# Late key products of a recurrence from turned keys, with their sums made by TensorE

## The reference, cut to what matters

```python
def ff_step(W, inp):                       # z of every row, known before the recurrence
    qt, kt, vt, bt = inp
    v_old = einsum('bhij,bhj->bhi', W, kt)
    W = W + (bt * (vt - v_old))[..., :, None] * kt[..., None, :]
    return (W, einsum('bhij,bhj->bhi', W, qt))

def rec_step(carry, inp):
    R, h = carry
    zt, kt, vt, bt = inp
    q_rec = softmax(h)                     # over the 32 of each head
    v_old = einsum('bhij,bhj->bhi', R, kt)
    R = R + (bt * (vt - v_old))[..., :, None] * kt[..., None, :]
    h = zt + einsum('bhij,bhj->bhi', R, q_rec)
    return ((R, h), h)
```

## Time and profile before

| | |
|---|---|
| time, median of 3 runs | 637.33 us (637.17 to 638.97) |
| time of the profiled execution | 636.17 us |
| its span | 634.3 us |
| TensorE busy | 565.3 us (89%) |
| VectorE busy | 428.2 us (68%) |
| ScalarE busy | 352.2 us (56%) |
| GpSimd busy | 349.7 us (55%) |
| recurrence, copy of state 0 to copy of state 15 | 262.54 to 439.13 us |

### The profile page before, as it was taken

One profiled execution on the slowest core, in us unless ns is written; L12 is line 12 of the kernel. 1 busy time (PEld: TensorE's weight loads), 2 busy tenths in 40 slices (PEclk: granted clock), 3 DMA queues, 4 the chain that ended last, 5 costly groups with the idle time before them and its releaser, 6 DMA issues.

```text
span 634.3 us, 12534 instructions
## 1 busy us (share of the span) xinstructions
PE 565.3 (89%) x4562; PEld 429.6 (68%) x4562; DVE 428.2 (68%) x1092; ACT 352.2 (56%) x915; POOL 349.7 (55%) x469
## 2 busy tenths in 40 slices
PE   7987999999999786679788878999999999999996
PEld 3556777778435675458777768787567778786686
DVE  4942663423877787799899878998414987766534
ACT  1272444444687674226688867770565577757530
POOL 2597563311450776788999899984366430001435
PEclk9998999999999998898999989999899999999998
DMA  8000000000000434200000000000000000000000
GB/s 281 7 1 1 2 0 1 1 1 1 1 1 2 71 81 67 78 0 2 2 1 1 1 2 1 2 1 0 2 1 1 3 2 2 1 2 2 9 9 17
DMA packets 10860, 10.43 MB, mean 16 GB/s; under 512 B 6000, under 2 KB 9840, under 8 KB 10544
## 3 DMA queue, kind: packets, MB, share of 16 engines
q1 hardware_dynamic: 8080, 7.54, 4.4%
q0 software_dynamic: 2144, 1.75, 1.7%
q10 hardware_dynamic: 576, 0.35, 0.3%
HBM read 5.77 MB, written 0.52 MB: 10 GB/s over the span
## 4 chain that ended last, share of the span: by engine, by line
PE 58%; DVE 17%; POOL 9%; ACT 7%; issue 4%; DMA 4%; SPq 1%; DVEq 0%; POOLq 0%; ACTq 0%
PE bank L1267 8%; PE bank L1347 8%; PE bank L1255 6%; PE bank L1612 5%; PE bank L1571 5%; DVE bank L2061 3%; DVE features L2055 2%; PE bank L1519 2%; PE bank L1658 2%; PE bank L1338 2%; PE bank L1307 2%; DMA coefs<-features 2%; POOL rstd L383 2%; PE bank L1317 2%; DVE features L2031 1%
## 5 line engine op out<-in xcount | busy, mean ns | idle before, releaser
L1347 PE MATMUL bank<-ident,features 128*128 128x128 f32 x604 | 80.7, 284 | 11.8 <-DVE features L2031 6.5
L1347 PEld LDWEIGHTS bank<-ident,features 128*128 128x128 f32 x604 | 71.1, 148 | 19.2 <-DVE features L2031 12.1
L855 ACT ACTIVATE G<-bank,cols 128x512 f32<-128x512 f32 x64 | 43.9, 686 | 54.3 <-PE bank L1255 54.3
L590 POOL TENSOR_TENSOR features<-UV,coefs 128x1024 f32<-128x1024 f32 (+3 forms) x36 | 59.6, 1672 | 2.7 <-DVE UV L2018 2.7
L1267 PE MATMUL bank<-weights,G 128*128 128x128 f32 x512 | 60.9, 278 | 0.0
L1267 PEld LDWEIGHTS bank<-weights,G 128*128 128x128 f32 x512 | 59.6, 195 | 0.0
L1255 PE MATMUL bank<-xs,weights 128*128 128x512 f32 x128 | 57.8, 594 | 0.9 <-ACT xs L846 0.9
L2031 DVE TENSOR_TENSOR features<-UV,bank 128x1024 f32<-128x1024 f32 (+3 forms) x68 | 55.6, 861 | 1.3 <-PE bank L1347 0.6
L390 POOL TENSOR_SCALAR rstd<-mv 128x4 f32<-128x4 f32 x8 | 1.5, 193 | 91.4 <-DVE mv L402 91.4
L940 ACT ACTIVATE xs<-UV,coefs 128x32 f32<-128x32 f32 x232 | 50.3, 308 | 0.0
L940 ACT ACTIVATE sx<-UV,coefs 128x32 f32<-128x32 f32 x200 | 43.4, 309 | 0.0
(11 more groups left out here) (356 smaller groups left out, 1397.2 us busy)
## 6 DMA issues: line engine op xcount, KB each, us to landing
weights<-in_w SPq DMA_DIRECT2D x2, 1024.0 KB, 9.4
features<-in_tok SPq DMA_DIRECT2D x1, 768.0 KB, 5.9
weights<-in_ew SPq DMA_DIRECT2D x4, 128.0 KB, 3.2
weights<-in_ew SPq DMA_DIRECT2D x2, 256.0 KB, 3.0
coefs<-G POOLq DMA_DIRECT2D x16, 25.5 KB, 5.0
rows<-in_rows SPq DMA_DIRECT2D x1, 384.0 KB, 6.3
out_h<-H SPq DMA_DIRECT2D x3, 128.0 KB, 2.0
coefs<-G SPq DMA_DIRECT2D x14, 25.5 KB, 5.0
```

The lines of the kernel that those rows point to most:

```text
L590: pool.tensor_tensor(out, u, co, ALU.mult).then_inc(s["held_p"], 1)
L855: act.activation(G[:, 4 * (w % 2) + f, :], up_bank(f)[:], ACT.Gelu, bias=col("b1", 4 * i + f)).then_inc(s["tok_gelu"], 1)
L1347: last = mm(out[:, P * k:P * k + P], x[:, P * k:P * k + P], ident[:], is_transpose=True, start=first and k == 0, stop=last_ and k == n - 1 ...
```

## The change

The eight late products are made from turned data. TensorE turns keys 4 to 11, one in each of steps 1 to 8 (`turn_keys_late`, two transposes into bank 0), and ScalarE copies each into SBUF (`turned_out`). In steps 10 to 15 the exponential is turned and copied in the same way. GpSimd multiplies the turned keys by the turned exponential; the 32 columns of a head are now 32 partitions. TensorE adds them with `key_sums`: for each product eight multiplications in which the product is the stationary operand and `heads4`, a block of ones for each head, 4 columns wide, is the moving one. VectorE no longer sums these products. It multiplies the sums by the reciprocal straight out of PSUM, in pieces (`shares`), and reads the late pieces last but one. `FIRST` becomes 4 instead of 2 in steps 11 to 14, and `SUMS_WARM` is smaller in steps 10, 12 to 15.

```diff
-FIRST = [min(t + 1, CH if t < 10 else 2) for t in range(T)]
+FIRST = [min(t + 1, 2 if t in (10, 15) else CH) for t in range(T)]
...
-SUMS_WARM = [0, 0, 3, 3] + [6] * 7 + [0] + [6] * 3 + [13]
+SUMS_WARM = [0, 0, 3, 3] + [6] * 6 + [3, 0, 3, 3, 0, 8]
+KEY_TURNS = 8
...
+def turns_until(t):
+    return 2 * NC + (t if t <= KEY_TURNS else KEY_TURNS + max(0, t - KEYS + 1))
...
 # GpSimd, key_products(t)
-                    pool.wait_ge(s["h_exp"], exps_of(t + 1))
+                    pool.wait_ge(s["rk_turned"], turns_until(t))
-                    pool.tensor_tensor(PD[:, j, :].rearrange("p (r x) -> p r x", r=CH), RK[:, CH * j:CH * j + CH, :],
-                                       expS[:].unsqueeze(1).broadcast_to([P, CH, HB]), ALU.mult)
+                    pool.tensor_tensor(PD[:, j, :].rearrange("p (r x) -> p r x", r=CH), keysT[j - 1],
+                                       expT.unsqueeze(1).broadcast_to([P, CH, HB]), ALU.mult)
...
 # ScalarE
+            def turned_out(t, out):
+                act.wait_ge(s["rk_T"], turns_until(t))
+                act.activation(out, bankKT, ACT.Copy).then_inc(s["rk_turned"], 1)
...
                 if t + 1 < T:
                     query_row(t + 1)
+                if 1 <= t <= KEY_TURNS:
+                    turned_out(t, keysT[(t - 1) // CH][:, (t - 1) % CH, :])
+                elif t >= KEYS:
+                    turned_out(t, expT)
+                if t + 1 < T:
                     half = {9: 2, 10: 2, 11: 3}.get(t, OWN[t + 1] // 2)
                     own_rows(t + 1, 0, half)
...
 # TensorE
+            def turn_keys_late(t):
+                x = RK[:, CH + t - 1, :] if t <= KEY_TURNS else expS
+                pe.wait_ge(s["e_sub"], t)
+                if t >= KEYS:
+                    pe.wait_ge(s["h_exp"], exps_of(t + 1))
+                for n in range(2):
+                    last = nc.tensor.transpose(bankKT[:, P * n:P * n + P], x[:, P * n:P * n + P], ident[:])
+                last.then_inc(s["rk_T"], 1)
+
+            def key_sums(t, j):
+                n = key_pieces(t).index(j)
+                pe.wait_ge(s["o_add"], t)
+                pe.wait_ge(s["key_p"], keys_until(t) + n + 1)
+                for r in range(CH):
+                    for k in range(2):
+                        x = HB * r + P * k
+                        last = mm(bankKS[j - 1][:, NH * r + 4 * k:NH * r + 4 * k + 4], PD[:, j, x:x + P], heads4,
+                                  start=True, stop=True)
+                last.then_inc(s["gram_mm"], 1)
...
                 own_reads(t)
+                if 1 <= t <= KEY_TURNS or t >= KEYS:
+                    turn_keys_late(t)
                 queries(t)
...
                 other_reads(t)
+                if t == 12:
+                    pe.wait_ge(s["o_add"], t)
+                    warm(SUMS_WARM[t])
                 if t + 1 < T:
                     held(t + 1)            # key_sums(t, 1) inside it, ahead of the third piece, for t = 11, 12
                     turn_held(t + 1)
-                if SUMS_WARM[t]:
+                if SUMS_WARM[t] and t != 12:
                     pe.wait_ge(s["o_add"], t)
                     warm(SUMS_WARM[t])
+                if t not in (11, 12):
+                    for j in key_pieces(t):
+                        key_sums(t, j)
                 read_out("rec", t, reads_of("rec", t))
...
 # VectorE, read_coefficients(t): shares(lo, hi, sums) multiplies by the reciprocal
-                for n, j in enumerate(key_pieces(t)):
-                    dve.wait_ge(s["key_p"], keys_until(t) + n + 1)
-                    summed(j)
-                ch.settle()
-                cr = bankCR[:, 0:t + 1, :]
-                ch(dve.tensor_tensor(cr, cr, smallv[:, 5, 0:NH].unsqueeze(1).broadcast_to([P, t + 1, NH]), ALU.mult))
+                k1 = CH * (len(key_pieces(t)) + 1)
+                for lo, hi in ((0, CH), (k1, t + 1)) if k1 > CH else ((0, t + 1),):
+                    shares(lo, hi, bankCR[:, lo:hi, :])
...
 # VectorE, step(t)
-                products("rec", t, reads_of("rec", t))
+                part = reads_of("rec", t)
+                late = len(key_pieces(t))
+                products("rec", t, part[:len(part) - late - 1])
+                for n, j in enumerate(key_pieces(t)):
+                    dve.wait_ge(s["gram_mm"], NH * NG + keys_until(t) + n + 1)
+                    shares(CH * j, CH * j + CH, bankKS[j - 1].rearrange("p (r h) -> p r h", r=CH))
+                ch.settle()
+                products("rec", t, part[len(part) - late - 1:])
...
+            ch(dve.tensor_reduce(heads4, ident[:].rearrange("p (h k) -> p h k", h=4), AX_X, ALU.add))
```

More of the change, by code:

```diff
@@ L71, in pieces @@
     return [(r, min(r + step, n)) for r in range(0, n, step)]
-FIRST = [min(t + 1, CH if t < 10 else 2) for t in range(T)]
+FIRST = [min(t + 1, 2 if t in (10, 15) else CH) for t in range(T)]
 def last_row_alone(n):
-    return pieces(n - 1) + [(n - 1, n)] if n > 1 else [(0, 1)]
+    if n <= KEYS:
+        return pieces(n - 1) + [(n - 1, n)] if n > 1 else [(0, 1)]
+    cuts = pieces(n - 1)
+    late = [(CH * j, CH * j + CH) for j in key_pieces(n - 1)]
+    return [c for c in cuts if c not in late] + late + [(n - 1, n)]
 def read_pieces():
@@ L88, in read_pieces, with key_pieces @@
     return out
+KEYS = 10
+KEYS2 = 14
+def key_pieces(t):
+    return [j for j, lo in ((1, KEYS), (2, KEYS2)) if t >= lo]
 READS = read_pieces()
@@ L110, in helds_of @@
     return [(i, r0, r1) for i, (x, r0, r1) in enumerate(HELDS) if x == t]
-SUMS_WARM = [0, 0, 3, 3] + [6] * 7 + [0] + [6] * 3 + [13]
-KEYS = 10
-KEYS2 = 14
+SUMS_WARM = [0, 0, 3, 3] + [6] * 6 + [3, 0, 3, 3, 0, 8]
+KEY_TURNS = 8
 def keys_until(t):
     return max(0, t - KEYS) + max(0, t - KEYS2)
-def key_pieces(t):
-    return [j for j, lo in ((1, KEYS), (2, KEYS2)) if t >= lo]
+def turns_until(t):
+    return 2 * NC + (t if t <= KEY_TURNS else KEY_TURNS + max(0, t - KEYS + 1))
 def exps_of(t):
@@ L239, in build @@
         bankER = bank[3][:, 0:HB]
+        bankKT = bank[0][:, HB:2 * HB]
+        bankKS = [bank[1][:, 128:160], bank[5][:, HB:HB + 32]]
+        keysT = [b.rearrange("p (r x) -> p r x", r=CH) for b in (w1f[:, 1024:2048], SX[:, 2320:3344])]
+        expT = FT[:, 12288:12544]
+        heads4 = smallv[:, 6, 8:12]
         tok = KKf[:, 0:N].bitcast(I32)
@@ L607, in key_products @@
                 if t >= KEYS:
-                    pool.wait_ge(s["h_exp"], exps_of(t + 1))
+                    pool.wait_ge(s["rk_turned"], turns_until(t))
                 for j in key_pieces(t):
-                    pool.tensor_tensor(PD[:, j, :].rearrange("p (r x) -> p r x", r=CH), RK[:, CH * j:CH * j + CH, :],
-                                       expS[:].unsqueeze(1).broadcast_to([P, CH, HB]), ALU.mult).then_inc(s["key_p"], 1)
+                    pool.tensor_tensor(PD[:, j, :].rearrange("p (r x) -> p r x", r=CH), keysT[j - 1],
+                                       expT.unsqueeze(1).broadcast_to([P, CH, HB]), ALU.mult).then_inc(s["key_p"], 1)
             def expert_bias(k):
@@ L1353, in held @@
                 for i, r0, r1_ in helds_of(t):
+                    if t in (12, 13) and r0 == 2 * CH:
+                        key_sums(t - 1, 1)
                     pe.wait_ge(s["held_p"], i + 1)
@@ L1379, in read_out @@
                     last.then_inc(s["read_mm"], 1)
+            def turn_keys_late(t):
[16 more added lines that the diff above has]
+                last.then_inc(s["gram_mm"], 1)
             def turn_state(t):
                 pe.wait_ge(s["hs_saved"], t + 1)
+                if t:
+                    pe.wait_ge(s["rk_turned"], turns_until(t))
                 if t:
@@ L2075, in read_coefficients, with shares @@
                         ch(dve.reciprocal(smallv[:, 5, 0:NH], smallv[:, 4, 0:NH]))
-                for n, j in enumerate(key_pieces(t)):
-                    dve.wait_ge(s["key_p"], keys_until(t) + n + 1)
-                    summed(j)
                 ch.settle()
-                cr = bankCR[:, 0:t + 1, :]
-                ch(dve.tensor_tensor(cr, cr, smallv[:, 5, 0:NH].unsqueeze(1).broadcast_to([P, t + 1, NH]), ALU.mult))
+                k1 = CH * (len(key_pieces(t)) + 1)
+                for lo, hi in ((0, CH), (k1, t + 1)) if k1 > CH else ((0, t + 1),):
+                    shares(lo, hi, bankCR[:, lo:hi, :])
                 ch.settle()
+            def shares(lo, hi, sums):
+                ch(dve.tensor_tensor(bankCR[:, lo:hi, :], sums,
+                                     smallv[:, 5, 0:NH].unsqueeze(1).broadcast_to([P, hi - lo, NH]), ALU.mult))
             def row_stats(t):
```

## The result

The changed kernel takes 652.28 us (median of 4 runs, 648.92 to 655.47), the one before 637.35: the ratio is 1.0234, 95% interval 1.0189 to 1.0279. The direction was forecast; the time lies 2.8 us above the range. The profiled execution took 648.92 us with a span of 647.2, so 12.75 us more than the one of before. It was the fastest of the four. In it the recurrence runs from 261.62 to 452.88 us: 14.7 us longer than before; what lies ahead of it and behind it was 0.9 us shorter each time.

A forecast was written before the change was run, and what follows sets the result against it. No single engine was taken to bound the recurrence. The step terms summed to +7.6 us on the profiled 636.17, giving 643.8; with 1.2 for the median 644.9, stated as 645, range 639.5 to 649.5 us.

The forecast's parts named there:

- What bounds each step, and VectorE's win: Recurrence: no single engine bounds it; VectorE's win counts only in steps 13 and 15, at most 2.7 us.
- Price of a key sum: TensorE's queue ahead of the reads: 16 instructions at 0.11 us, 1.8 us a sum, bounds 0.9 and 3.5.
- rival of cheap sums: TensorE's key sums: moving columns set the pace, a sum costs next to nothing; 638 us, chance 0.05.
- ScalarE's stall: Copies of turned data delay ScalarE's own rows: +1.1, +1.4, +0.6, +0.9 us in steps 6, 7, 8, 10.
- Steps 11 to 15: Late recurrence: step 11 -2.2 us, clock included, then +1.0, +1.0, +2.9 and +0.6 us in steps 12 to 15.
- Steps 1 to 5: Early recurrence: few own rows and ScalarE idles, so +0.3 us in all, bounds 0 and 1.
- The clock: Step 11: key sums shorten TensorE's longest pause to near 1 us, the clock stays at 1.00, -1.8 us.
- the clock falls elsewhere: Steps 6 and 7: TensorE's idling drops the clock, 1.6 to 1.8 us a fall; 647 to 650 us, chance 0.20.
- The other side: Faster rival: ScalarE isn't held up, steps 6 to 10 cost nothing; 632 to 637 us, chance 0.08.

The follow-up runs named there:

- e10: Kernel before the change with only the new `FIRST` and five warm-up calls in TensorE's pause of step 11: ratio 0.9947, median 632.91 us.
- e4: Changed kernel with the second half of the heads left out of the key sums: ratio 1.0171 to the kernel before, median 646.25 us.
- e5: Changed kernel with key sums multiplying by 128 columns, zeros behind the first four, instead of 4: ratio 1.0164 to the kernel before, median 646.71 us.
- e1: Changed kernel with copies of turned keys in steps 1 to 8 moved behind the copy of the sum of v_old: ratio 1.0152 to the kernel before, 643.04 us.
- e12: Changed kernel run once more, with nothing altered: the profiled execution took 655.43 us.
- e3: Changed kernel with five more warm-up calls in step 7 and three in step 14, in TensorE's pause: ratio 1.0159 to the kernel before, 644.77 us.
- e7: Changed kernel with 128-column key sums, turned keys copied later, turned exponentials behind one own row, no warm-up from step 10: ratio 1.0003 to the kernel before, 636.44 us.
- e9: Kernel before the change, warm-up of steps 14 and 15 made of twice as many instructions with 4 columns: ratio 1.0041, median 638.98 us.

## Why the prediction was right in direction and wrong in size

- *What bounds each step, and VectorE's win.* Right. Eight sums left VectorE and no step from 10 to 15 got shorter by it: at full clock each takes 0.2 to 2.9 us more than in e10, which has the new `FIRST` and VectorE's own sums. VectorE waits for TensorE's sums instead, 3.71 and 3.21 us in step 14 of the profile. e4 shows that TensorE's queue ends last in steps 14 and 15.
- *Price of a key sum, 1.8 us.* Right: 32 pieces in 3.63 us in step 15, 0.11 each, and 0.12 with 128 moving columns (e5). The moving columns don't set this pace, and the rival of cheap sums falls. The Trainium skill (TensorE: Matmul & The Clock Gate, section "Step-by-step: what each phase is for") says that the time of a weight load scales with the columns of the weights. The trace fits that, as all these pieces load 128 columns; no run here varies the columns of the weights.
- *ScalarE's stall.* Right in mechanism and size: 1.05, 1.26, 0.42 and 0.82 us in steps 6, 7, 8 and 10, forecast 1.1, 1.4, 0.6 and 0.9; e1 takes the first three away.
- *Steps 11 to 15 at full clock.* -2.15, +0.93, +0.77, +2.87 and +0.61 us measured; -2.2, +1.0, +1.0, +2.9 and +0.6 forecast. Steps 1 to 5 gave -0.1 for +0.3, but the kernel before spent 3.4 us at 0.50 in step 4, where its time was 9.75 us; against 9.35 in e1 at 1.00 the stall costs 0.3 there, as forecast. The sum of the column at full clock is +6.5 us, and some +6.9 with that step 4 set right, where mine was +7.6.
- *The clock: the step that failed.* "With key sums in the gap TensorE's longest pause is near 1 us; I take back 1.8 us (bounds 0 and 1.8)." I priced the clock by pauses alone and took sums on a busy TensorE for cover. The pause came out as I said and the clock fell all the same: in step 11 of the profile the longest pause is 0.86 us, ahead of the key sum, and the clock falls behind that sum (it does so in e12 too; in e3, with the same pause and sum, it holds).

```profile
374.52 1.92 PE L1428 MATMUL bank<-smallv,features 128*128 128x4 f32 x16 [0.86 <-POOL features L627]
```

Narrow sums are followed by 0.50 without any pause (step 15), and wide ones of the same duration hold 1.00 (e5). In the profiled execution the clock gave back 0.6 of the 1.8 us in step 11 and took 1.7 in step 7, 4.2 in step 14 and 1.1 in step 15: with the 1.2 that step 11 didn't give back, 8.2 us over the sum at full clock. That execution was the fastest of the four, and by itself it would lie 0.6 us inside the range; the median lies 3.4 us above it, and e12 shows such a slower execution with more time at 0.50. The rival "the clock falls elsewhere" named steps 6 and 7 rightly, but priced each fall at 1.6 to 1.8 us, where step 14 lost 4.2, had none in steps 13 to 15 and ended at 650. Its chance of 0.20 was far too low, and the range was too low with it.
- *The other side.* That ScalarE isn't held up was wrong at once. Even with its stall cut, wide sums and no late warm-up (e7) the change is only level with the kernel before.

What stays open: which execution falls in which of the steps with a pause. Of steps 6 to 8 the same kernel fell in step 7 alone in one profile and in all three in the next, with the same pauses of 2.60, 2.38 and 1.94 us; no run here tells why. Nor does one tell why step 14 fell for 10.2 us in the first profile and for 3.4 in the next.

## What to carry to other kernels

A copy that waits for another engine is placed in a queue behind the work that someone else waits for, not ahead of it: moving eight copies by a few lines gave back 3 us at full clock (0.3 in step 4, 2.7 in steps 6 to 8). When work goes from VectorE to TensorE, price it in TensorE's queue at the rate of its weight loads, in each step where TensorE ends last, and ask what the new instructions do to the granted clock, not only how long they are. Filling a pause that ends in a fall of the clock was worth more here than moving sums: five warm-up calls in step 11 gave 1.5 us there, and with the new `FIRST` the kernel is 0.5% faster.

## What the runs showed of the hardware that was not expected

TensorE's granted clock fell from 1.00 to 0.50, from 2.4 to 1.2 GHz, while or after TensorE worked, without a pause that the profile shows, on instructions with 128 columns of weights and 4 moving columns: in e9 in the midst of 52 of them (6.69 us), in step 15 of the changed kernel behind 32 of them (3.63 us). The same 32 with 128 moving columns, at 0.12 us each, kept 1.00 (e5). From step 6 on each microsecond at 0.50 cost about half a microsecond (13.6 us more at 0.50, 6.7 us longer, e12); that accounts for the 6.5 us between the two profiled executions of the changed kernel, 648.92 and 655.43 us.
